# Normalisation moved from VectorE to ScalarE, low parts moved within a unit, and a bias folded into the products of a graph pass

## The chip, the cores and the metric

The kernel runs on one core of a Trainium2 chip. The metric is the device time of one execution in microseconds (us); lower is better. Three executions of the kernel before were timed, and one more was taken with the hardware profiler.

## The reference

`x` is 128 graphs of 64 nodes with 384 features, `adj` is 128 matrices of 64x64. Four layers follow each other, each as `x = layernorm(x + layer(x, adj))`:

- Layers 0 and 3: attention with 12 heads over the 64 nodes of a graph; the adjacency (twice it in layer 0) is added to the scaled scores; then an output projection with its bias.
- Layer 1: attention with 12 heads, `beta * adj` added, scores where `adj` is not over 0 masked; no output projection.
- Layer 2: two inner layers of a graph network. Each takes `softmax(h h^T / sqrt(384)) * adj`, normalised by its row sums, as `attn`, and

```
ctx = (attn * upper) @ (h Wl^T + bl) + diag(attn) * (h Ws^T + bs) + (attn * lower) @ (h Wr^T + br)
h = relu(layernorm(ctx) * g + beta)
```

All is float32.

## The kernel before

The 8192 rows are cut into 16 groups of 512 rows, and a group into 4 units of 128 rows (two graphs). There are five passes over all rows, one after the other, with a barrier of all engines between them: `attention_pass` for layer 0 (first pass), for layer 1 (second pass), `digcn_pass` for the two inner layers (first and last graph pass), and `attention_pass` for layer 3 (last pass). Rows go to memory between passes. Each pass writes its own queue for every engine by hand: a function `group(i, pair, par)` per engine lists, unit by unit (`s` = 0 to 3, `n` the unit's number), what the engine does, and the engines meet at semaphores. Within an engine's queue everything is done in the order written. Most operands have two buffers, `b` = 0 and 1.

Products are made of a high and a low part: every matrix and every row block is rounded to the format of the fast matmul (the high part, an operation of ScalarE) and what the rounding loses is kept as a second matrix (the low part, a subtraction). A product is then nine matmuls, three over the depth for each of high-high, low-high and high-low (`SPLIT`).

In an attention pass a unit `n` goes this way:

- PE: `scores(n)` (L471), `values(n-2)` (L505 or L509), the transposes of the probabilities `probs_T(n-1)` (L484), the output projection `output(n-2)` (L524, where `wo` is set: first and last pass), and between them the ten projections of the next group (`ahead`, L444 and L450), spread over the four units by `BETWEEN`. They wait for the next group's high and low parts.
- DVE (VectorE): `residual(n-3)` (L807 adds the rows, L811 and L814 take mean and variance), `softmax_max(n)` (L751, L758, in first and last pass L760), `low_part(n-2)` (L794 or L798), `normed(n-3)` (L823: subtract the mean, multiply by the inverse deviation), in unit 2 `edges` (L738, L740 or L743), `softmax_sum(n)` (L765 to L780), then transposes of later rows (L717) and, in first and last pass, their low parts (L723).
- POOL (GpSimd): `rstd(n-3)` (L339, L341: the inverse deviation), the subtraction of the maximum (L387), `value_bias(n)` (L347); in the second pass then `add_rows(n-2)` (L366) and `rows_low` (L372: in unit 2 two low parts, in unit 3 one); in first and last pass `output_bias` (L355) and the multiplication L398, which waits for L776.
- ACT (ScalarE): evacuates the projections from PSUM, `exp(n)` (L656), `probs_T` (L651), `values` (L666), high parts (L584).
- The SP queue loads rows and stores `yo`; a store waits for the normalisation of its unit.

In a graph pass (`digcn_pass`; `ends` is true in the last one alone) a unit `n` goes this way:

- PE: projections LEFT and RIGHT (L1165), `context(n-1)` (L1179), in unit 1 `products` of the next group (L1138, they wait for the transposes L1332), the projection SELF (L1165), in unit 3 `attention_T` of the next group (L1149, it waits for L1372).
- DVE: `itself(n-1)` (L1386: SELF plus its bias row into `hs`), transposes (L1332: unit 0 one, units 2 and 3 one each), in unit 3 attention steps 3 and 4 (L1366, L1372, L1377, L1379: the last makes `diag`), `inner_norm` (L1412 to L1425 if `ends`, else L1428 and L1434), `context(n-1)` (L1398: `hs * diag + ps_c`, then L1401 and L1404), in unit 1 step 0, in unit 2 steps 1 and 2 (L1352, L1355, L1358, L1361).
- ACT: `left_right` (L1242), high parts, exp, `standardise(n-2)` (L1259) and `normed(n-4)` (L1267) if `ends`, else `relu`.
- POOL: inverse deviations (L1070 to L1076), low parts (L1085), `side_biases` (L1092), attention steps (L1052, L1058).

## Time and profile before

| | |
|---|---|
| median of 3 runs | 2729.84 us (2726.38 to 2730.54) |
| profiled execution | 2732.55 us |
| its span, first to last instruction | 2730.8 us |
| mean granted clock of TensorE | 0.966 |
| PE busy | 2468.6 us (90%) |
| DVE busy | 2263.7 us (83%) |
| POOL busy | 1895.4 us (69%) |
| ACT busy | 1456.9 us (53%) |
| DMA, mean | 74 GB/s |

Busy time is given per engine over the whole span; the passes have different limits, so the shares are averages over five unlike stages. The view of windows gives the same for a stretch, the view of the timeline gives single instructions with their start and duration in us and, in square brackets, the idle time of their engine just before them and what ended it. An arrow `out<-in` names the operands; `l_` stands for the pass.

### The profile page before, as it was taken

The page shows a single profiled execution, that of the slowest core. Times are in us where ns is not written, and L with a number is a line of the kernel's source. Part 1 is how long each engine was busy: PE and PEld are TensorE (multiplying, and loading weights), DVE is VectorE, ACT ScalarE, POOL GpSimd, SP SyncE. Part 2 cuts the span into 40 slices and gives each one's busy share as a digit, 9 for nine tenths or more (in the row PEclk, how much of TensorE's full clock was granted, in tenths as well). Part 3 has the DMA queues.
Part 4 walks back from the last instruction along what each step waited for, and adds up shares of the span by engine and source line. Part 5 has one row for each costly group of instructions (what it writes and reads, how often), then busy time and mean ns, then how long its engine had stood idle before and what let it go on. Part 6 is the DMA issues. An engine that isn't in the chain of part 4 may idle for free. (4 is left out here: it accounts for less than half of the span.)

```text
span 2730.8 us, 64297 instructions
## 1 busy us (share of the span) xinstructions
PE 2468.6 (90%) x21490; PEld 2094.7 (77%) x21490; DVE 2263.7 (83%) x3822; ACT 1456.9 (53%) x2964; POOL 1895.4 (69%) x2093
## 2 busy tenths in 40 slices
PE   6999999995999999959999978998895999999997
PEld 5888888874877777748888867777774788888886
DVE  5999999984788888867777769889897699999997
ACT  4555555552666666535544545555554555555553
POOL 2777777773677777756666647788784577777776
PEclk9999999997999999979999989999997999999999
DMA  7222222115233332163332163333324222222211
GB/s 133 62 66 70 70 66 70 47 46 104 63 80 76 90 76 66 54 125 72 73 67 64 50 114 83 89 91 76 92 65 95 49 66 70 67 68 70 58 45 51
DMA packets 320740, 200.89 MB, mean 74 GB/s; under 512 B 243440, under 2 KB 320624, under 8 KB 320624
## 3 DMA queue, kind: packets, MB, share of 16 engines
q1 hardware_dynamic: 320624, 199.40, 31.6%
q8 instruction: 66, 1.08, 0.2%
q14 instruction: 50, 0.41, 0.0%
HBM read 136.42 MB, written 62.91 MB: 73 GB/s over the span
## 5 line engine op out<-in xcount | busy, mean ns | idle before, releaser
L450 PE MATMUL l_ps_p<-l_xT,l_w 128*128 128x512 f32 x2304 | 602.7, 409 | 99.6 <-POOL l_xT L372 50.4
L1165 PE MATMUL l_ps_h<-l_w,l_hT 128*128 128x384 f32 x3456 | 658.1, 345 | 10.1 <-DVE l_hs L1386 7.3
L1165 PEld LDWEIGHTS l_ps_h<-l_w,l_hT 128*128 128x128 f32 x3456 | 607.1, 191 | 74.0 <-issue 42.4
L450 PEld LDWEIGHTS l_ps_p<-l_xT,l_w 128*128 128x128 f32 x2304 | 430.9, 193 | 197.1 <-issue 102.2
L387 POOL TENSOR_TENSOR l_pr<-l_sc,l_st 128x768 f32<-128x768 f32 x192 | 283.1, 1475 | 328.8 <-DVE l_st L758 327.6
L347 POOL TENSOR_TENSOR v<-v,l_bvs 128x768 f32<-128x768 f32 x192 | 375.6, 1956 | 0.0
L1242 ACT ACTIVATE l_hlr<-l_ps_h 64x384 f32<-64x384 f32 x512 | 248.8, 486 | 228.3 <-PE l_ps_h L1165 219.1
L1092 POOL TENSOR_TENSOR l_hlr<-l_hlr,l_sides 128x768 f32<-128x768 f32 x128 | 240.1, 1876 | 119.9 <-ACT l_hlr L1242 119.9
L444 PE MATMUL l_ps_p<-l_w,l_xT 128*128 128x384 f32 x1584 | 311.2, 342 | 0.0
L615 ACT ACTIVATE v<-l_ps_p 64x192 f32<-64x192 f32 x704 | 228.6, 325 | 142.0 <-PE l_ps_p L444 135.3
L765 DVE TENSOR_REDUCE l_st<-l_pr 128x12 f32<-128x768 f32 x192 | 182.7, 952 | 126.9 <-ACT l_pr L656 125.7
L524 PE MATMUL l_ps_y<-l_w,l_oT 128*128 128x384 f32 x1152 | 237.6, 352 | 47.2 <-DVE l_oT L798 43.5
L444 PEld LDWEIGHTS l_ps_p<-l_w,l_xT 128*128 128x128 f32 x1584 | 273.1, 188 | 5.8 <-issue 0.2
L524 PEld LDWEIGHTS l_ps_y<-l_w,l_oT 128*128 128x128 f32 x1152 | 204.6, 193 | 80.9 <-issue 77.3
L398 POOL TENSOR_TENSOR l_pr<-l_pr,l_st 128x768 f32<-128x768 f32 x128 | 211.1, 1649 | 38.0 <-DVE l_st L776 28.6
L656 ACT ACTIVATE l_pr<-l_pr 128x768 f32<-128x768 f32 x192 | 163.1, 850 | 85.4 <-POOL l_pr L387 81.4
L751 DVE SCALAR_TENSOR_TENSOR l_sc<-l_ps_s,l_sbias 128x768 f32<-128x768 f32 x192 | 183.6, 956 | 30.1 <-PE l_ps_s L471 22.3
L651 ACT ACTIVATE l_pT<-l_ps_t 128x512 f32<-128x512 f32 (+1 forms) x384 | 167.5, 490 | 50.0 <-PE l_ps_t L484 44.4
L758 DVE TENSOR_REDUCE l_st<-l_sc 128x12 f32<-128x768 f32 x192 | 183.0, 953 | 6.7
L605 ACT ACTIVATE l_k<-l_ps_p,even_odd 128x512 f32<-128x512 f32 x192 | 121.7, 685 | 110.9 <-PE l_ps_p L450 110.9
L471 PE MATMUL l_ps_s<-l_k,l_qT 64*64 64x128 f32 x4608 | 172.1, 280 | 5.3 <-DVE l_sc L751 5.3
L484 PE MATMUL l_ps_t<-ident,l_pr 128*128 128x128 f32 x1152 | 165.5, 281 | 12.6 <-POOL l_pr L398 9.5
(127 smaller groups left out, 4297.9 us busy)
## 6 DMA issues: line engine op xcount, KB each, us to landing
rows<-l_yo SPq DMA_DIRECT2D x256, 192.0 KB, 1.9
l_xa<-rows SPq DMA_DIRECT2D x256, 192.0 KB, 4.3
l_xr<-rows SPq DMA_DIRECT2D x192, 192.0 KB, 2.4
l_xa<-in_x SPq DMA_DIRECT2D x64, 192.0 KB, 4.2
l_xr<-in_x SPq DMA_DIRECT2D x64, 192.0 KB, 2.4
out<-l_yo SPq DMA_DIRECT2D x64, 192.0 KB, 1.9
l_edge<-in_adj SPq DMA_DIRECT2D x80, 128.0 KB, 2.4
raw<-in_L_gnn_Wq SPq DMA_DIRECT2D x12, 144.0 KB, 4.8
```

Source lines behind the costliest of these rows:

```text
L347: nc.gpsimd.tensor_tensor(got, got, bvs[:, :, :].unsqueeze(1).to_broadcast([P, GPU, PAIRS, 64]), ALU.add).then_inc(pool_v, 1)
L387: nc.gpsimd.tensor_tensor(pr[b][:, :, :], sc[b][:, :, :], st[b][:, 0, :].unsqueeze(2).to_broadcast([P, HEADS, NODES]), ALU.subtract).then_ ...
L398: nc.gpsimd.tensor_tensor(pr[b][:, :, :], pr[b][:, :, :], st[b][:, 5, :].unsqueeze(2).to_broadcast([P, HEADS, NODES]), ALU.mult).then_inc( ...
L444: last = nc.tensor.matmul(bank[:, :D], rows[:, l, t, o * P:(o + 1) * P], W[2][:, r, t, :], start=c + t == 0, stop=c == 2 and t == KT - 1)
L450: last = nc.tensor.matmul(bank[:, :], W[m][:, l, t, o * P:(o + 1) * P], rows[:, r, t, :], start=c + t == 0, stop=c == 2 and t == KT - 1)
L524: last = nc.tensor.matmul(ps_y[:, :D], oT[b][:, l, t, :], W[3][:, r, t, :], start=c + t == 0, stop=c == 2 and t == KT - 1)
L615: i = nc.scalar.activation(v2[gpar][64 * odd:64 * odd + 64, GPU * u + g2, :, 32 * odd:32 * odd + 32], got[:, :, odd, :], ACT.Copy)
L751: nc.vector.scalar_tensor_tensor(out=sc[b][:, :, :], in0=logits[:, :, :NODES], scalar=scale, in1=sbias[par][:, s, :].unsqueeze(1).to_broad ...
L758: nc.vector.tensor_reduce(st[b][:, 0, :], sc[b][:, :, :], AX.X, ALU.max).then_inc(dve_mx, 1)
L1092: nc.gpsimd.tensor_tensor(hlr[b][:, :, :], hlr[b][:, :, :], sides[:, :, :], ALU.add).then_inc(pool_h, 1)
L1165: last = nc.tensor.matmul(ps_h[m][:, :D], hT[gpar][:, l, t, s * P:(s + 1) * P], W[m][:, r, t, :], start=c + t == 0, stop=c == 2 and t == K ...
L1242: i = nc.scalar.activation(hlr[b][half * NODES:(half + 1) * NODES, g, :], ps_h[m][g * NODES:(g + 1) * NODES, :D], ACT.Copy)
```

## The change

- All three attention passes: `normed` leaves DVE's queue and becomes three operations on ACT, which stand behind `exp(n)` and the evacuations next to it, and ahead of `rows_high`. The store and the reuse of `res` wait for ACT instead of DVE.
- Second pass: `rows_low` on POOL stands behind `rstd(n-3)` at the head of units 2 and 3, ahead of the subtraction of the maximum. In first and last pass low parts stay on DVE as they were.
- Last graph pass: the bias row of SELF is added by a tenth matmul (a matrix `pick` with rows 0 and 32 set to one, times a matrix `bias` whose rows 0 and 32 hold the high and the low part of the bias); ACT multiplies the result by `diag` while it reads it from PSUM into `hs`; DVE's `itself` is gone and its context sum is a plain addition.
- Both graph passes: DVE's order within a unit. In the last one it is context, attention steps 3 and 4, inner norm, transpose, steps 0 to 2; in the first one `itself`, steps 3 and 4, inner norm, context, transpose, steps 0 to 2.
- At the start of the kernel DVE fills `pick`.

The diff, cut to its core:

```diff
@@ constants, DVE
+                nc.vector.memset(self.pick[:, :].bitcast(F32), 0.0).then_inc(c_pick, 1)
+                dve.wait_ge(c_pick, 1)
+                dve.wait_ge(c_const, 5)
+                for row in (0, 32):
+                    nc.vector.tensor_copy(self.pick[row:row + 1, :], self.ones[row:row + 1, :]).then_inc(c_const, 1)
@@ attention_pass, POOL
                     rstd(n - 3, 1 - b)
+                    for t in ((), (), (0, 1), (2,))[s]:
+                        rows_low(i + 2, par, t)
                     pool.wait_ge(dve_mx, n + 1)
...
                         add_rows(n - 2, pair * 4 + 2 * par + s // 2 - 1, b)
-                        for t in ((), (), (0, 1), (2,))[s]:
-                            rows_low(i + 2, par, t)
@@ attention_pass, ACT
+            def normed(n, count, b):
+
+                if not inside(n, units):
+                    return
+                act.wait_ge(dve_mv, n + 1)
+                nc.scalar.activation(ln[b][:, 10:11], ln[b][:, 6:7], ACT.Copy, scale=-1.0).then_inc(act_nm, 1)
+                act.wait_ge(pool_rs, n + 1)
+                act.wait_ge(act_nm, 2 * n + 1)
+                nc.scalar.activation(ln[b][:, 11:12], ln[b][:, 10:11], ACT.Copy, scale=ln[b][:, 9:10]).then_inc(act_nm, 1)
+                act.wait_ge(act_nm, 2 * n + 2)
+                if counted(16 * count):
+                    act.wait_ge(s_out[b], 16 * count)
+                nc.scalar.activation(yo[b][:, :], res[b][:, :], ACT.Identity, bias=ln[b][:, 11:12],
+                                     scale=ln[b][:, 9:10]).then_inc(act_y, 1)
...
                         exp(n, s % 2)
                         fill(i, par, s, 1)
+                    normed(n - 3, pair * 4 + 2 * par + (s - 3) // 2, 1 - s % 2)
                     for t in ((), (0, 1), (2,), ())[s]:
                         rows_high(i + 2, par, t)
@@ attention_pass, DVE
                     low_part(n - 2, s % 2)
-                    normed(n - 3, count, 1 - s % 2)
@@ digcn_pass, PE
+                if ends and m == SELF:
+                    if isinstance(n, int) and n == 0:
+                        pe.wait_ge(c_row, 2)
+                    last = nc.tensor.matmul(ps_h[m][:, :D], pick[:, :], bias[:, :], start=False, stop=True)
@@ digcn_pass, ACT
                     normed(n - 4, pair * 4 + 2 * par + s // 2 - 2, b)
+                    if ends:
+                        act.wait_ge(pe_h, 3 * n + 3)
+                        act.wait_ge(dve_dg, i + 1)
+                        if counted(n - 1):
+                            act.wait_ge(dve_c, n - 1)
+                        nc.scalar.activation(hs[b][:, :], ps_h[SELF][:, :D], ACT.Copy,
+                                             scale=diag[par][:, s:s + 1]).then_inc(act_h, 1)
@@ digcn_pass, DVE
+                if ends:
+                    dve.wait_ge(act_h, 3 * (n + 1))
+                    nc.vector.tensor_tensor(c0[b][:, :], ps_c[:, :D], hs[b][:, :], ALU.add).then_inc(dve_c, 1)
...
+            if ends:
+                dve.wait_ge(act_w, steps + 1)
+                nc.vector.tensor_tensor(bias[32:33, :], brow[32:33, :], bround[32:33, :].bitcast(F32),
+                                        ALU.subtract).then_inc(c_row, 1)
...
+                    before = (i, par, s - 1) if s else (i - 1, 1 - par, UNITS - 1)
+                    if ends:
+                        context(n - 1, *before)
                     itself(n - 1, 1 - b)
+                    if s == 3:
+                        attention(i + 1, 1 - par, 3)
+                        attention(i + 1, 1 - par, 4)
+                    if ends:
+                        inner_norm(n - 3, pair * 4 + 2 * par + (s - 3) // 2, 1 - b)
+                    else:
+                        inner_norm(n - 2, pair * 4 + 2 * par + s // 2 - 1, b)
+                        context(n - 1, *before)
```

## Rows read from the trace of the kernel before

**Rows 1.** Windows, busy us of PE, PEld, DVE, ACT, POOL; passes one to four.
```profile
200.00:571.20 371.20, 361.37 (x3427) 306.29 (x3425) 339.46 (x551) 208.49 (x440) 272.36 (x241) 1.00 0.25 63
...
800.00:1049.00 249.00, 233.89 (x2422) 194.81 (x2422) 216.92 (x295) 153.84 (x317) 192.19 (x183) 0.99 0.33 80
...
1300.00:1497.00 197.00, 197.00 (x1408) 170.97 (x1407) 149.52 (x297) 98.68 (x200) 129.41 (x137) 1.00 0.31 69
...
1750.00:1981.00 231.00, 206.35 (x1404) 175.09 (x1403) 207.73 (x387) 128.21 (x231) 187.39 (x326) 0.97 0.35 84
```

**Rows 2.** Timeline (start us, duration us) of the first pass, one unit, DVE and POOL.
```profile
352.69 0.61 DVE L823 TENSOR_SCALAR l_yo<-l_res,l_ln 128x384 f32<-128x384 f32 x1
353.99 0.95 DVE L765 TENSOR_REDUCE l_st<-l_pr 128x12 f32<-128x768 f32 x1 [0.70 <-ACT l_pr L656]
...
355.24 0.76 DVE L776 SCALAR_TENSOR_TENSOR l_st<-l_st 128x12 f32<-128x12 f32 x1
...
353.04 1.97 POOL L347 TENSOR_TENSOR v<-v,l_bvs 128x768 f32<-128x768 f32 x1
354.97 1.02 POOL L355 TENSOR_TENSOR l_xr<-l_xr,l_bos 128x384 f32<-128x384 f32 x1
```

**Rows 3.** Timeline of POOL in the first unit of the first pass.
```profile
51.30 1.85 POOL L347 TENSOR_TENSOR v<-v,l_bvs 128x768 f32<-128x768 f32 x1
```

**Rows 4.** Groups of ACT by line (count, busy us, mean ns), the two graph passes.
```profile
L1259 ACT ACTIVATE l_c<-l_c,l_ln 128x384 f32<-128x384 f32 x64 | 45.1, 704 | 48.9 <-POOL l_ln L1076 48.7
...
L1251 ACT ACTIVATE l_yo<-l_c 128x384 f32<-128x384 f32 x64 | 33.0, 515 | 13.6 <-DVE l_c L1434 13.6
```

**Rows 5.** Timeline of the second pass, end of a group, POOL, DVE and PE.
```profile
920.43 1.48 POOL L387 TENSOR_TENSOR l_pr<-l_sc,l_st 128x768 f32<-128x768 f32 x1 [1.24 <-DVE l_st L758]
...
923.76 1.06 POOL L366 TENSOR_TENSOR l_res<-l_scaled,l_xr 128x384 f32<-128x384 f32 x1
...
926.14 0.50 DVE L811 BATCH_NORM_STATS2 l_ln<-l_res 128x6 f32<-128x384 f32 x1
...
933.36 1.25 POOL L372 TENSOR_TENSOR l_xT<-l_xF,l_xT 128x512 fp32r<-128x512 f32 x1
...
934.75 4.44 PE L450 MATMUL l_ps_p<-l_xT,l_w 128*128 128x512 f32 x18 [2.13 <-POOL l_xT L372]
```

**Rows 6.** Timeline of DVE in the last graph pass, units 0, 2 and 3.
```profile
1856.15 0.52 DVE L1412 TENSOR_TENSOR l_c<-l_c,l_gain 128x384 f32<-128x384 f32 x1
...
1858.97 0.62 DVE L1398 SCALAR_TENSOR_TENSOR l_c<-l_hs,l_diag,l_ps_c 128x384 f32<-128x384 f32 x1
...
1860.41 0.56 DVE L1386 TENSOR_TENSOR l_hs<-l_ps_h,l_own 128x384 f32<-128x384 f32 x1
...
1872.31 0.39 DVE L1352 TENSOR_REDUCE l_st<-l_u 128x4 f32<-128x256 f32 x1
...
1873.53 1.34 DVE L1358 SCALAR_TENSOR_TENSOR l_st<-l_st 128x4 f32<-128x4 f32 x1
...
1875.01 0.56 DVE L1386 TENSOR_TENSOR l_hs<-l_ps_h,l_own 128x384 f32<-128x384 f32 x1
...
1876.11 0.90 DVE L1366 TENSOR_TENSOR l_attn<-l_u,l_st 128x256 f32<-128x256 f32 x1
1877.04 0.70 DVE L1372 TENSOR_TENSOR l_wide<-l_attn,l_halves 128x512 f32<-128x512 f32 x1
```

**Rows 7.** Timeline of PE in the last graph pass, the context products of three units.
```profile
1862.01 0.87 PE L1179 MATMUL l_ps_c<-l_hlr,l_aT 128*64 128x384 f32 x4
...
1869.09 0.87 PE L1179 MATMUL l_ps_c<-l_hlr,l_aT 128*64 128x384 f32 x4
...
1874.90 0.54 PE L1179 MATMUL l_ps_c<-l_hlr,l_aT 128*64 128x384 f32 x2
```

**Rows 8.** Timeline of PE and DVE at the start of the last graph pass.
```profile
1625.81 0.60 PE L1149 MATMUL l_ps_a<-ident,l_wide 128*128 128x128 f32 x4
...
1626.68 0.52 DVE L1386 TENSOR_TENSOR l_hs<-l_ps_h,l_own 128x384 f32<-128x384 f32 x1
```

More of the change, by code:

```diff
@@ L904, in digcn_pass @@
         loaded = list(shared.loads)
-        own = a.sb("own", [P, D])
+        own = None if ends else a.sb("own", [P, D])
+        if ends:
+            pick = shared.pick
+            brow = a.sb("brow", [P, D])
+            bround = a.sb("bround", [P, D], F32R)
+            bias = a.sb("bias", [P, D], F32R)
+            c_zero, c_row = a.sem("c_zero"), a.sem("c_row")
         sides = a.sb("sides", [P, GPU, D])
@@ L982, in _ @@
             sp.dma_start(edge[0][:, :, :], adj_g[0]).then_inc(s_edge[0], 16)
-            sp.dma_start(own[:, :], row_biases[SELF].to_broadcast([P, D])).then_inc(s_small, 16)
+            if ends:
+                for row in (0, 32):
+                    sp.dma_start(brow[row:row + 1, :], row_biases[SELF]).then_inc(s_small, 16)
+            else:
+                sp.dma_start(own[:, :], row_biases[SELF].to_broadcast([P, D])).then_inc(s_small, 16)
             for g in range(GPU):
@@ L1157, in project @@
                     pe.wait_ge(dve_w, KT * (m + 1))
-                if m == SELF:
+                if m == SELF and not ends:
                     if counted(n):
                         pe.wait_ge(dve_s, n)
-                elif counted(2 * (n - 1) + m + 1):
-                    pe.wait_ge(act_h, 2 * (n - 1) + m + 1)
+                elif counted(taken * (n - 1) + m + 1):
+                    pe.wait_ge(act_h, taken * (n - 1) + m + 1)
                 for c, (l, r) in enumerate(SPLIT):
@@ L1381, in itself @@
             def itself(n, b):
-                if not inside(n, units):
+                if ends or not inside(n, units):
                     return
@@ L1435, in inner_norm @@
                                                op0=ALU.mult, op1=ALU.add).then_inc(dve_o, 1)
+            if ends:
+                nc.vector.memset(bias[:, :].bitcast(F32), 0.0).then_inc(c_zero, 1)
             weights(LEFT)
@@ L1479, in _ @@
             itself(units - 1, 1)
+            context(units - 1, groups - 1, 1, UNITS - 1)
             if ends:
                 inner_norm(units - 3, units // 2 - 2, 1)
-            context(units - 1, groups - 1, 1, UNITS - 1)
             inner_norm(units - 2, units // 2 - 1, 0)
```

64 lines of the change are left out of this document (31 added, 33 removed).

## The prediction, made before the changed kernel was run

> **What bounds the kernel now.** I first read busy time in one steady stretch of each pass [rows 1], each of whole groups (a group is four 128-row units): 371.2/10 = 37.1 us a group in the first pass, 249/8 = 31.1 in the second, 197/8 = 24.6 in the first graph pass, 231/8 = 28.9 in the last. The last pass repeats the first (37.1). TensorE is busy 361.37 of 371.2, all of 197, but only 206.35 of 231. So the first graph pass is bound by TensorE, and a faster VectorE gives nothing there; the last graph pass does the same products with 4.3 us a group more, and VectorE is busy 207.73 of 231.
>
> Then the order in time of one unit of the first pass [rows 2]. VectorE never waits for TensorE in it; it waits 0.70 us for ScalarE's exp (L765). That wait closes a chain: maximum on VectorE, subtraction on GpSimd, exp on ScalarE, sum on VectorE. The normalisation (L823) stands inside that wait. The second thing to see is L776: a 128x12 operation that takes 0.76 us and ends at 356.00, when GpSimd's L355 (354.97 + 1.02) ends at 355.99. GpSimd's sequence after the maximum sets VectorE's next step, so VectorE's busy share hides two waits, not one.
>
> In the second pass TensorE waits 2.13 us once a group for the low part L372, which ends at 934.61 [rows 5]. It looks like the prize, but no wait of VectorE for TensorE stands in the steady stretch: TensorE idles because VectorE's and GpSimd's chain paces it.
>
> **Part 1: normalisation to ScalarE (three passes, 192 units).** Off VectorE goes L823. In units 0, 1, 3 of a group the exp wait grows by what is removed: 0.70 becomes about 1.3, gain 0. What does transfer is small: GpSimd's L347 takes 1.97 behind L823 [rows 2] and 1.85 in the first unit, where there is no L823 yet [rows 3]. L355 and L776 come 0.12 earlier. In unit 1 that is lost, as TensorE's and ScalarE's evacuations lead into unit 2's exp; units 0 and 3 keep it: 2 x 0.12 x 32 groups of the first and last pass = -7.7. Bounds: 0 and 3 x 0.12 x 32 = -11.5.
>
> On ScalarE come three operations: a 128x384 one with scale and bias columns, 0.704, of which the same size without them is 0.515 [rows 4]; and two of one element per partition, priced between 0 and 0.515 each, and taken as 0.2, as most of the 384 elements are gone. With two waits on its own results, some 0.15 together, about 1.25 us a unit, 240 us in all. In the first pass ScalarE is busy 208.49 of 371.2 [rows 1]; with 40 x 1.25 = 50 more it is idle less and is not full. The normalisation stands behind exp, so it can't delay it; behind it are queued the high parts and the last evacuation of the unit. I take nothing for it; if the cover is gone, the excess is paid twice a group. Against it speaks the Trainium skill, "ScalarE: Activation LUTs", section "Rules for kernel authors", which puts adds and multiplies on VectorE, not ScalarE. By its rule the exchange is a loss in busy time (the trace agrees: 0.704 against 0.61); what decides is the wait that covers it.
>
> Ends: at the end of each attention pass the last store waits for 0.2 + 0.704 instead of 0.61 on the path: 3 x 0.3 = +0.9.
>
> **Part 2: low parts at a unit's head in the second pass.** The two or one L372 (1.25 each, [rows 5]) move ahead of GpSimd's subtraction L387 in units 2 and 3. In unit 2 that one waits 1.24 us for the maximum, 2.5 us of low parts go in, so the subtraction is 1.3 us late, and with it exp, value bias and L366. L366 now ends at 924.82, its reader L811 starts at 926.14: the slack of 1.3 us is used up exactly. VectorE's own way to L811 leads through the edge operations, whose two also wait for GpSimd; with L823 gone they start 1.5 earlier. In unit 3 1.25 us meet a similar wait. Unit 2: +0.2, unit 3: 0, less 0.1 for the faster L347. Sum 0. TensorE's 2.13 us wait goes, and comes back elsewhere as it waits for exp. Bounds: -0.5 and +2.0 us a group (no slack used at all), -8 to +32.
>
> **Part 3: last graph pass.** VectorE loses the bias addition L1386 (0.56) four times a group, 2.2 us, and the context sum becomes a plain addition, 0.05 cheaper: 2.4 a group. ScalarE gains one scaled read of PSUM, 4 x 0.6, onto 128.21/8 = 16.0; TensorE one more matmul a unit, which at 5.81 for a unit's 31 [rows 7] is 0.19, 0.8 a group. If VectorE's sum were all, the group would be 26.5. But the order changes too: context first, then attention steps 3 and 4, inner norm, and the transpose last. Where a product starts the next context, waits close a loop across engines. I add it up from TensorE's context of unit 2:
> - context to VectorE's start 0.9;
> - context 1.45 (1858.97 to 1860.41), inner norm 2.82 (1856.15 to 1858.97), its wait for GpSimd's side biases 0.7, transpose 0.63, attention 1 and 2 at 1.5: L1352 starts at 1872.31 and L1386 at 1875.01, 2.70, of which L1358 holds 1.34 where it needs about 0.16 [rows 6]; together 7.1;
> - in unit 3 context 1.45 and L1366, L1372 at 1.15 (1876.11 to 1877.74 is 1.63 with a stall): 2.6;
> - TensorE's attention transpose and two projections: 4.0;
> - unit 0 to 1: 5.81 (1869.09 to 1874.90) + 0.19; unit 1 to 2: 7.08 (1862.01 to 1869.09) + 0.19 [rows 7]; 13.3.
>
> Sum 27.9, against 28.9: -1.0 x 16 = -16. TensorE then waits for `wide` instead of for the context. Bounds: 26.5 (-38) and, with L1358 stalled as in [rows 6] and more, 29.6 (+11). I take 27.9 as it has every stall but the one that hangs on a few hundredths.
> At its start VectorE subtracts the bias row behind its transposes, at about 1626.7, and TensorE's attention transpose, which stood at 1625.81 [rows 8], follows unit 0's SELF product: +1.3 with the waits.
>
> **Part 4: nothing.** In the first graph pass the transpose moves behind the context; TensorE is full there [rows 1] and needs it a unit later. The constants at the start of the kernel: +0.5 (0 to 1).
>
> **Sum:** -7.7 - 16 + 0.9 + 1.3 + 0.5 = -21. Profiled execution 2732.55 (span 2730.8 and 1.75 around it), so 2711.5; it stood 2.7 above the median 2729.84, so 2709. 0.2% is 5.5 us, about what a measurement can tell here.
>
> **Rivals.**
> A, forecast, 54%.
> B, the stall in the last graph pass. L1358, 1.34 us in [rows 6], is issued in my schedule within 0.1 us of GpSimd's side biases. If it comes second, the group is 29.6 and `wide` later: -21 + 27 = +6, 2736. For it: L776 in [rows 2] shows the same waiting to the end of another engine's operation. The Trainium skill, "SBUF — State Buffer", section "Who interferes with whom", says the same: an operation of VectorE with two SBUF inputs and one of GpSimd exclude each other, and issue order decides. 14%.
> C, the loop isn't closed and VectorE's sum counts: 26.5 a group, -38 in place of -16, 2687. For it: in the old order VectorE hardly waits for TensorE there. Against it: the new order ties `wide` to the context. 17%.
> D, slower: in the second pass the late subtraction isn't hidden. It decides where L366 ends later than L780, from 1.3 us a group on, which eats the 21; at 2.0 us a group +32, so +11, 2741. Against it the slack counted above. 10%.
> E, slower too: ScalarE is late. At the upper bounds the three operations take 0.704 + 2 x 0.515 and some 0.3 of waits, 2.0 us rather than 1.25, and the evacuations queued behind them come late; 0.75 x 2 x 48 groups = +72, less 21, 2781. Against it: ScalarE is idle 44% of the first pass. 5%. The page on ScalarE named in part 1 has the rule that leads here.
> That the diff doesn't do what its title says I see no room for, beside that "stay" means no edit.
>
> **Numbers.** Faster: C and nearly all of A, 70%. Same: half of B, the edge of A and D, 13%. Slower: 17%. The range 2683 to 2737 takes in A, B and C and leaves D and E out.
>
> **What would show it.** First pass: L765's wait near 1.3 where it was 0.70, L347 at 1.85, group 36.9. Second: group 31.1 still, no wait for L372, L811 waiting for L366. Last graph pass: group 27.9, TensorE waiting for L1372's successor, no wait for the context sum. Wrong: the second pass shorter by over 0.5 us a group (then TensorE did pace it), or the graph pass near 26.5 or 29.6.

## The result, and the profile after

The changed kernel is slower: 2750.48 us (2749.3 to 2753.89, four runs) against 2728.54 us (2726.38 to 2730.54, four runs) of the kernel before on the same chip, a ratio of 1.0081, 95% interval 1.0069 to 1.0093. The forecast was 2709, range 2683 to 2737. Of the two profiled executions the spans differ by 18.1 us (2730.8 and 2748.9), as the one before stood some 4 us above its median.

The page of the kernel after: span, and busy time of each engine.
```profile
span 2748.9 us, 65175 instructions
...
PE 2478.1 (90%) x21554; PEld 2101.8 (76%) x21554; DVE 2095.0 (76%) x3571; ACT 1698.2 (62%) x3606; POOL 1878.9 (68%) x2093
```
VectorE was given less to do, and nothing gained by it. To see where the time went I cut the span at ScalarE's exp instructions, 64 in each attention pass (their starts in the timeline):

| stretch, us | before | after |
|---|---|---|
| start to first exp | 51.5 | 50.8 |
| first pass, exp 1 to 64 | 574.1 | 582.4 |
| to the second pass | 65.9 | 64.7 |
| second pass, exp 1 to 64 | 487.1 | 481.4 |
| both graph passes | 956.7 | 965.9 |
| last pass, exp 1 to 64 | 577.4 | 584.1 |
| to the end | 18.1 | 19.6 |

So three stretches lost (8.3, 9.2 and 6.7 us), one gained (5.7). How much such a stretch varies by itself is read from the kernels below in which its pass is as before: 573.8 to 574.1 us for the first pass, 487.1 to 488.4 for the second, 956.4 to 958.1 for the graph passes, 574.3 to 577.4 for the last. Windows of the kernel after that answer to the first, second and last of [rows 1] (PE, PEld, DVE, ACT, POOL, granted clock):
```profile
200.00:571.20 371.20, 355.52 (x3396) 301.54 (x3395) 308.54 (x503) 250.07 (x553) 263.32 (x237) 1.00 0.25 62
...
800.00:1049.00 249.00, 234.81 (x2451) 193.40 (x2450) 173.89 (x265) 188.82 (x417) 191.11 (x185) 1.00 0.34 80
...
1750.00:1981.00 231.00, 209.22 (x1363) 178.89 (x1362) 187.03 (x350) 137.60 (x257) 184.79 (x317) 0.96 0.35 83
```
In the first and last of these TensorE got through fewer matmuls than in [rows 1], 3396 against 3427 and 1363 against 1404; in the second through more, 2451 against 2422.

**First pass.** Timeline of VectorE and GpSimd in one unit after, the counterpart of [rows 2]. L791 was L765, L796, L799 and L802 were L770, L773 and L776, L354 and L362 were L347 and L355.
```profile
358.21 0.95 DVE L791 TENSOR_REDUCE l_st<-l_pr 128x12 f32<-128x768 f32 x1 [1.23 <-ACT l_pr L663]
359.08 1.02 DVE L796 SCALAR_TENSOR_TENSOR l_st<-l_st 128x12 f32<-128x12 f32 x1
360.02 0.21 DVE L799 RECIPROCAL l_st<-l_st 128x12 f32<-128x12 f32 x1
360.27 0.17 DVE L802 SCALAR_TENSOR_TENSOR l_st<-l_st 128x12 f32<-128x12 f32 x1
...
357.25 1.84 POOL L354 TENSOR_TENSOR v<-v,l_bvs 128x768 f32<-128x768 f32 x1
359.04 1.04 POOL L362 TENSOR_TENSOR l_xr<-l_xr,l_bos 128x384 f32<-128x384 f32 x1
```
The value bias L354 takes 1.84 us and not 1.97, as forecast. So the output bias L362 begins at 359.04, and VectorE's 128x12 operation L796, issued at 359.08, lasts until that one ends: 1.02 us. The row of the same operation in the kernel before stands between those of [rows 2]:
```profile
354.86 0.17 DVE L770 SCALAR_TENSOR_TENSOR l_st<-l_st 128x12 f32<-128x12 f32 x1
```
In both kernels the sum begins 0.95 us behind the value bias (0.96 after) and the small operation 1.82 us behind it (1.83 after). But the output bias began 1.93 us behind it before and begins 1.79 us behind it now. Before, the first two of the three got through and only the last was caught (0.76 us, of which 0.6 waiting); now the first is caught and the other two follow it, and the last of them ends 3.19 us behind the start of the value bias instead of 2.96.

This is not one unit's accident. In each of the two passes 45 of the 64 units have the output bias beside that small operation (units 0, 1 and 3 of a group). Before, VectorE's was issued first in all 90, by 0.12 us at most (mostly 0.10), and took 0.16 to 0.18 us. After, it was issued second in all 90, by 0.01 to 0.09 us, and took 0.96 to 1.04.

**Second pass.** Unit 2 of a group after: GpSimd's low parts L379 (L372) and subtraction of the maximum L396 (L387), VectorE's maximum L784, sum L791 and the first operation of the variance, L839 (L811).
```profile
924.15 2.55 POOL L379 TENSOR_TENSOR l_xT<-l_xF,l_xT 128x512 fp32r<-128x512 f32 x2
926.65 1.53 POOL L396 TENSOR_TENSOR l_pr<-l_sc,l_st 128x768 f32<-128x768 f32 x1
...
924.31 0.95 DVE L784 TENSOR_REDUCE l_st<-l_sc 128x12 f32<-128x768 f32 x1
...
929.10 0.95 DVE L791 TENSOR_REDUCE l_st<-l_pr 128x12 f32<-128x768 f32 x1 [0.63 <-ACT l_pr L663]
...
931.19 0.56 DVE L839 BATCH_NORM_STATS2 l_ln<-l_res 128x6 f32<-128x384 f32 x1 [0.88 <-POOL l_res L373]
```
The maximum is there at 925.26; the subtraction starts 1.39 us later, behind the low parts, and VectorE waits for exp even in the unit of the edge operations. Then it waits 0.88 us more for GpSimd's addition of the rows (L373, before L366): what rival D of the prediction described.

**Last graph pass.** Timeline of VectorE and TensorE at a group's turn after (L1445 was the context sum L1398, L1410 and L1416 the attention steps L1366 and L1372, L1176 the attention transpose L1149), three windows over it, and from the views of TensorE's and of VectorE's waits between 1800 and 1980 us the largest of each.
```profile
1912.21 0.56 DVE L1445 TENSOR_TENSOR l_c<-l_ps_c,l_hs 128x384 f32<-128x384 f32 x1
...
1913.57 0.54 DVE L1410 TENSOR_TENSOR l_attn<-l_u,l_st 128x256 f32<-128x256 f32 x1
1914.14 0.70 DVE L1416 TENSOR_TENSOR l_wide<-l_attn,l_halves 128x512 f32<-128x512 f32 x1
...
1914.89 0.66 PE L1176 MATMUL l_ps_a<-ident,l_wide 128*128 128x128 f32 x4 [2.48 <-DVE l_wide L1416]
1915.75 4.96 PE L1192 MATMUL l_ps_h<-l_w,l_hT 128*128 128x384 f32 x18 [0.20 <-issue]
```
```profile
1913.00:1916.00 3.00, 0.90 (x5) 0.67 (x6) 2.79 (x8) 0.73 (x2) 2.73 (x5) 0.97 0.00 0
1916.00:1919.00 3.00, 3.00 (x10) 3.00 (x10) 2.43 (x5) 0.18 (x1) 0.78 (x3) 0.50 0.19 49
1919.00:1922.00 3.00, 3.00 (x16) 2.15 (x16) 0.27 (x1) 2.87 (x6) 0.30 (x2) 0.96 0.22 82
```
```profile
PE l_ps_a L1176 <- DVE l_wide L1416: 14.4, 6, 2.5
...
DVE l_c L1445 <- PE l_ps_c L1211: 14.2, 13, 2.9
```
The same view of TensorE's waits in the kernel before:
```profile
PE l_ps_c L1179 <- DVE l_c L1398: 10.5, 6, 1.9
...
PE l_ps_a L1149 <- DVE l_wide L1372: 1.5, 6, 0.3
```
The wait of 0.25 us for `wide` has become one of 2.48, since the context sum now stands in front; the wait for the context sum is gone. Behind this wait the granted clock is 0.50, the lower of its two levels (1.2 GHz), and 18 matmuls take 4.96 us; such a row of 18 takes 3.29 at a clock of 1.00. And VectorE, which takes the context sum first, now stands waiting for TensorE's context (14.2 us). A group, from one attention transpose to the next, takes 29.8 us on average; by the same reading it was 29.2 before, not the 28.9 that the prediction took from a window. The clock doesn't fall in each group: of ten between 1720 and 2020 us it does in seven. These seven take 30.1 us on average, the three at a clock of 1.00 take 29.1 (the one from 1886.09 to 1914.89 takes 28.8, the next one, with this fall, 30.6). The kernel before has such falls too, in six of ten groups, behind its waits of 1.6 to 1.9 us for the context sum; I had not looked. But they cost nothing there: its groups take 28.9 and 29.5 us in turn, whether the clock falls in them (28.91 from 1760.98, 29.52 from 1848.27) or not (28.89 from 1877.79, 29.50 from 1965.08).

### The profile page after: what moved, and what is told of

It is laid out like the page before. It is cut to its first block and busy times, and to the rows that moved or that the text cites. A ratio compares the mean times of both kernels' runs of the same rounds, so it can differ in the third digit from the quotient of the medians.

```text
span 2748.9 us, 65175 instructions
## 1 busy us (share of the span) xinstructions
PE 2478.1 (90%) x21554; PEld 2101.8 (76%) x21554; DVE 2095.0 (76%) x3571; ACT 1698.2 (62%) x3606; POOL 1878.9 (68%) x2093
## 5 line engine op out<-in xcount | busy, mean ns | idle before, releaser
L1192 PE MATMUL l_ps_h<-l_w,l_hT 128*128 128x384 f32 x3456 | 671.5, 347 | 2.2 <-issue 2.0
L1192 PEld LDWEIGHTS l_ps_h<-l_w,l_hT 128*128 128x128 f32 x3456 | 614.0, 193 | 63.3 <-issue 53.9
L457 PEld LDWEIGHTS l_ps_p<-l_xT,l_w 128*128 128x128 f32 x2304 | 425.2, 191 | 175.9 <-issue 86.0
L396 POOL TENSOR_TENSOR l_pr<-l_sc,l_st 128x768 f32<-128x768 f32 x192 | 284.0, 1479 | 298.9 <-DVE l_st L784 298.9
L791 DVE TENSOR_REDUCE l_st<-l_pr 128x12 f32<-128x768 f32 x192 | 182.9, 953 | 289.5 <-ACT l_pr L663 289.5
L354 POOL TENSOR_TENSOR v<-v,l_bvs 128x768 f32<-128x768 f32 x192 | 358.0, 1865 | 0.0
L1119 POOL TENSOR_TENSOR l_hlr<-l_hlr,l_sides 128x768 f32<-128x768 f32 x128 | 249.1, 1946 | 123.3 <-ACT l_hlr L1274 122.8
L784 DVE TENSOR_REDUCE l_st<-l_sc 128x12 f32<-128x768 f32 x192 | 183.0, 953 | 6.6
L478 PEld LDWEIGHTS l_ps_s<-l_k,l_qT 64*64 64x64 f32 x4608 | 125.9, 134 | 64.7 <-issue 58.0
```

The source lines that it names most:

```text
L354: nc.gpsimd.tensor_tensor(got, got, bvs[:, :, :].unsqueeze(1).to_broadcast([P, GPU, PAIRS, 64]), ALU.add).then_inc(pool_v, 1)
L396: nc.gpsimd.tensor_tensor(pr[b][:, :, :], sc[b][:, :, :], st[b][:, 0, :].unsqueeze(2).to_broadcast([P, HEADS, NODES]), ALU.subtract).then_ ...
L457: last = nc.tensor.matmul(bank[:, :], W[m][:, l, t, o * P:(o + 1) * P], rows[:, r, t, :], start=c + t == 0, stop=c == 2 and t == KT - 1)
L478: last = nc.tensor.matmul(logits[g * NODES:(g + 1) * NODES, h:h + 2, :NODES], qT[par][q, t, c:c + NODES], k2[par][q, t, :, c:c + NODES], s ...
L1119: nc.gpsimd.tensor_tensor(hlr[b][:, :, :], hlr[b][:, :, :], sides[:, :, :], ALU.add).then_inc(pool_h, 1)
L1192: last = nc.tensor.matmul(ps_h[m][:, :D], hT[gpar][:, l, t, s * P:(s + 1) * P], W[m][:, r, t, :], start=c + t == 0, stop=not (ends and m = ...
```

## The experiments

Each was timed in five rounds beside the kernel before, which took 2730.8 us beside e1 to e4, 2729.4 beside e5, e7, e8 and e9, and 2730.3 beside the rest. The ratio is to these. The columns of the table are the stretches of the one above: first pass, second pass, both graph passes, last pass.

| kernel | us | ratio (95% interval) | first | second | graph | last |
|---|---|---|---|---|---|---|
| e1_norm | 2725.77 | 0.9982 (0.9973 to 0.9991) | 582.0 | 468.6 | 956.6 | 583.7 |
| e2_low | 2731.57 | 1.0000 (0.9991 to 1.0009) | 574.0 | 488.6 | 956.9 | 575.8 |
| e3_graph | 2741.64 | 1.0034 (1.0021 to 1.0048) | 573.8 | 488.1 | 968.5 | 575.8 |
| e4_wide_first | 2743.89 | 1.0043 (1.0030 to 1.0057) | 574.0 | 488.2 | 970.4 | 574.4 |
| e5_old_order | 2713.97 | 0.9938 (0.9925 to 0.9952) | 573.9 | 487.2 | 939.6 | 575.3 |
| e6_bias_ahead | 2703.77 | 0.9903 (0.9887 to 0.9918) | 562.6 | 488.4 | 958.1 | 564.7 |
| e7_norm_bias_ahead | 2685.95 | 0.9837 (0.9823 to 0.9850) | 563.8 | 468.7 | 956.4 | 562.9 |
| e8_later_T | 2729.30 | 0.9997 (0.9988 to 1.0006) | 573.8 | 487.6 | 954.7 | 575.7 |
| e9_norm_mid | 2710.48 | 0.9928 (0.9915 to 0.9942) | 573.8 | 469.2 | 957.5 | 574.3 |
| e10_best | 2670.06 | 0.9782 (0.9769 to 0.9796) | 562.7 | 468.2 | 940.9 | 563.8 |
| e11_low_back | 2739.38 | 1.0031 (1.0018 to 1.0043) | 582.3 | 468.1 | 971.2 | 584.1 |
| e12_spare | 2711.38 | 0.9928 (0.9915 to 0.9942) | 573.9 | 468.3 | 956.5 | 574.3 |

### Single parts of the change: e1_norm, e2_low, e3_graph

**e1_norm**
```diff
 # before, attention_pass, DVE
-                    normed(n - 3, count, 1 - s % 2)
 # ACT, behind exp
+                    normed(n - 3, pair * 4 + 2 * par + (s - 3) // 2, 1 - s % 2)
```


> Of the change only the normalisation on ScalarE in the three attention passes; low parts and graph passes as before. Theory T1 (the whole of the loss in the first and last pass is this part: GpSimd's value bias runs in 1.85 us instead of 1.97, its output bias then starts just ahead of VectorE's subtraction m0, which waits it out at about 1.02 us instead of 0.17, and the sum over heads and the residual follow later): first and last pass +7 to +9 us each (a group 37.1 to about 37.6), second pass between -3 and 0, both graph passes unchanged; whole kernel +9 to +17 us, 2738 to 2746. Rival (the loss in these passes is something else, and the part gives what was forecast): -8 us, 2721. Rival (ScalarE is late with the evacuations behind its three new instructions): also slower, but then PE waits for ScalarE's evacuations grow and m0 stays at 0.17.

Measured 2725.77: 5 us faster, so T1's time for the whole kernel (9 to 17 us slower) was missed, and the rival's gain of 8 us was not reached. The first and last pass lost 7.9 and 6.3 us, about as T1 had it. The second pass gained 18.5, which neither theory had. Its cause stands in unit 2 of a group. First the kernel before, VectorE's timeline, then ScalarE's exp:
```profile
920.64 1.47 DVE L823 TENSOR_SCALAR l_yo<-l_res,l_ln 128x384 f32<-128x384 f32 x1
922.04 1.92 DVE L738 TENSOR_SCALAR l_off<-l_edge 128x256 f32<-128x256 f32 x1
923.99 1.11 DVE L740 SCALAR_TENSOR_TENSOR l_sbias<-l_edge,l_betas,l_off 128x256 f32<-128x256 f32 x1
925.02 0.94 DVE L765 TENSOR_REDUCE l_st<-l_pr 128x12 f32<-128x768 f32 x1
...
921.93 0.85 ACT L656 ACTIVATE l_pr<-l_pr 128x768 f32<-128x768 f32 x1 [1.05 <-POOL l_pr L387]
```
The same of e1_norm, where the edge operations are L757 and L759, the sum L784:
```profile
948.28 1.40 DVE L757 TENSOR_SCALAR l_off<-l_edge 128x256 f32<-128x256 f32 x1
949.72 1.95 DVE L759 SCALAR_TENSOR_TENSOR l_sbias<-l_edge,l_betas,l_off 128x256 f32<-128x256 f32 x1
951.59 0.94 DVE L784 TENSOR_REDUCE l_st<-l_pr 128x12 f32<-128x768 f32 x1
...
949.57 0.85 ACT L656 ACTIVATE l_pr<-l_pr 128x768 f32<-128x768 f32 x1 [0.70 <-POOL l_pr L387]
```
In this unit VectorE doesn't wait for exp: its own work holds the sum up, until 2.24 us after exp's end before (922.78 to 925.02) and 1.17 after it now (950.42 to 951.59). 1.07 us a group times 16 is 17 of the 18.5. And L823 took 1.47 us there, until 0.2 us behind the end of GpSimd's L387 (921.91, [rows 5]). So it was a wait too. The 0.61 of [rows 2] holds a shorter one: there also L823 ends 0.21 us behind the end of L387 (353.09), and in the last three units of each attention pass, where no operation of GpSimd overlaps it, it takes 0.48. The Trainium skill, "SBUF — State Buffer", section "Who interferes with whom", says that an operation of this kind, one tensor with scalars, can take the pair of ports that VectorE shares with GpSimd; the rows agree (1.47 us beside L387, 0.48 with nothing beside it).

**e2_low**
```diff
 # before, attention_pass, POOL
                     rstd(n - 3, 1 - b)
+                    for t in ((), (), (0, 1), (2,))[s]:
+                        rows_low(i + 2, par, t)
                     pool.wait_ge(dve_mx, n + 1)
...
                         add_rows(n - 2, pair * 4 + 2 * par + s // 2 - 1, b)
-                        for t in ((), (), (0, 1), (2,))[s]:
-                            rows_low(i + 2, par, t)
```


> Of the change only the subtraction of the low parts at the head of a unit in the second pass; everything else as before. Theory: TensorE's wait of 2.13 us for the last low part goes, the group stays within 0.3 us of 31.1; the second pass between -6 and +1 us, the other stages unchanged, whole kernel 2722 to 2730. Rival D of the prediction (the add of the rows comes late behind the subtractions): second pass +8 or more, 2737 or more.

Measured 2731.57, within a microsecond of before; the second pass took 488.6 us, 0.5 more than in e3_graph and e4_wide_first, where it is untouched. The wait for the low part went (15.1 us in eight waits between 800 and 1049 us before), waits for ScalarE and VectorE came in its place (7.1 and 6.6 us), and nothing was gained, as forecast. The range stated was missed by 1.6 us, the mechanism held.

**e3_graph**
```diff
 # attention passes as before; Shared and digcn_pass as after
+                    if ends:
+                        context(n - 1, *before)
```


> Attention passes as before; the last graph pass (and what it shares) as in the changed kernel: the bias as a matmul, the scaling on ScalarE, the new order on VectorE. Theory T2: TensorE waits 2.2 to 2.6 us a group for the transpose wide, which now stands behind the context sum on VectorE, and after that wait its granted clock falls to between 0.6 and 0.8; a group 30.1 instead of 28.9, whole kernel +8 to +11 us, 2737 to 2740. Rival (the last graph pass only suffers from the state in which the attention pass leaves the cores): the pass is faster than before here, 2712 to 2725.

Measured 2741.64, 11 us more and 1.6 above the range of T2, all in the graph stretch (968.5 against 956.7). A group takes 29.9 us, TensorE waits 2.3 to 2.7 for `wide`, and the clock falls in eight of ten groups. The rival, that the pass suffers from something before it, falls. The three parts alone come to -5, +1 and +11 us, +7 in all; the change cost 22. So two of them don't add up.

### Why the first and last pass lost: e12_spare, e7_norm_bias_ahead, e6_bias_ahead

**e12_spare**
```diff
 # e1_norm, first and last pass, DVE, at the old place
+                nc.vector.tensor_scalar(spare[b][:, :], res[b][:, :], ln[b][:, 6:7], ln[b][:, 9:10], ALU.subtract,
+                                        ALU.mult).then_inc(dve_spare, 1)
```


> As e1_norm, and in the first and last pass VectorE also computes the normalisation at its old place, into a spare tile that nobody reads: 61 instructions of 0.61 us more in each of these passes, while ScalarE keeps its three new ones. Theory T1 (the passes are longer because without that instruction GpSimd's value bias ends 0.12 us earlier and the output bias is under way before m0 is issued): value bias 1.97 us again, m0 at 0.17, the first and last pass back at 574 and 575 us though VectorE does more; whole kernel 2709 to 2716. Rival (ScalarE's three instructions are what is late): the passes stay at 582 and 584 us or grow by VectorE's 0.6 us a unit, 2724 or more.

Measured 2711.38, 14 us faster than e1_norm with 122 instructions more. Timeline of VectorE (L845 writes the spare tile, L790 is the small operation) and GpSimd (L348 value bias, L356 output bias):
```profile
352.34 0.61 DVE L845 TENSOR_SCALAR l_spare<-l_res,l_ln 128x384 f32<-128x384 f32 x1
...
354.52 0.17 DVE L790 SCALAR_TENSOR_TENSOR l_st<-l_st 128x12 f32<-128x12 f32 x1
...
352.69 1.96 POOL L348 TENSOR_TENSOR v<-v,l_bvs 128x768 f32<-128x768 f32 x1
354.62 1.01 POOL L356 TENSOR_TENSOR l_xr<-l_xr,l_bos 128x384 f32<-128x384 f32 x1
```
The small operation is again 0.10 us ahead of the output bias instead of 0.04 behind it, and the passes are back at 573.9 and 574.3. ScalarE has its three new instructions here too; so it isn't ScalarE. A useless instruction, worth 0.61 us of VectorE's time a unit, pays for itself by making GpSimd's value bias 0.12 us longer.

**e7_norm_bias_ahead**
```diff
 # e1_norm, attention_pass, POOL
                     rstd(n - 3, 1 - b)
+                    output_bias(n - 2, pair * 4 + 2 * par + s // 2 - 1, b)
                     pool.wait_ge(dve_mx, n + 1)
...
-                    output_bias(n - 2, pair * 4 + 2 * par + s // 2 - 1, b)
                     pool.wait_ge(dve_rinv, n + 1)
```


> As e1_norm, and in the first and last pass GpSimd's output bias stands ahead of its wait for the maximum instead of behind the value bias. Theory T1: the subtraction m0 that e1_norm holds up for about 1.0 us and the two instructions behind it are free (m0 at 0.17 us), the first and the last pass lose the 6 to 8 us that e1_norm added and up to 12 us more each; whole kernel 2686 to 2714. Rival (the passes are late for ScalarE's three new instructions and not for the collision): the passes stay at e1_norm's 582 and 584 us, 2722 or more. Rival (the bias ahead of the wait delays GpSimd's subtraction of the maximum by its 1.0 us): slower than e1_norm, 2735 or more.

Measured 2685.95, at the lower edge of T1's range (2686). The output bias (L355) now runs in GpSimd's idle time, and nothing meets the small operations (L789 is the first of them). Timeline of POOL and DVE, and the only line that the view of TensorE's waits has between 210 and 560 us:
```profile
352.67 1.01 POOL L355 TENSOR_TENSOR l_xr<-l_xr,l_bos 128x384 f32<-128x384 f32 x1
...
358.90 0.16 DVE L789 SCALAR_TENSOR_TENSOR l_st<-l_st 128x12 f32<-128x12 f32 x1
```
```profile
PE l_ps_y L524 <- DVE l_oT L817: 3.2, 9, 0.4
```

**e6_bias_ahead**: the same move in the kernel before, the normalisation still on VectorE.


> The kernel before with one change: in the first and last pass GpSimd's output bias stands ahead of its wait for the maximum. Theory T1 (the gain of e7 is the collision of the output bias with the three small VectorE instructions, of which before only the last, 0.6 us over its own length, was caught): units 0, 1 and 3 of a group 0.4 to 0.7 us shorter, the two passes 8 to 20 us less each, whole kernel 2692 to 2714. Rival (the order gains only with the normalisation off VectorE): within 4 us of before, 2725 to 2733.

Measured 2703.77, in the range of T1, and the rival falls: the passes take 562.6 and 564.7 us. Against e7 (563.8, 562.9) the normalisation's place makes no difference to them once the collision is gone; TensorE bounds them then: it is busy 346.6 of the 350 us between 210 and 560 in both. The whole of what the change cost in these passes, and 12 us a pass beyond it, lay in where GpSimd adds 128x384 numbers.

### The second pass: e9_norm_mid, e11_low_back

**e9_norm_mid**: `normed` on ScalarE where `wo` is not set, on VectorE where it is.


> Of the change only the normalisation on ScalarE, and that in the second attention pass alone; all else as before. Since e1_norm lost 8 and 6 us in the first and last pass and gained 18.5 us in the second: second pass 467 to 471 us between its first and last unit (487.1 before), first and last pass as before (574, 577), whole kernel 2708 to 2716. Rival (the second pass gains because the first leaves it another state): second pass over 480, 2724 or more.

Measured 2710.48; the second pass took 469.2. The gain is the pass's own.

**e11_low_back**
```diff
 # after, attention_pass, POOL
                     rstd(n - 3, 1 - b)
-                    for t in ((), (), (0, 1), (2,))[s]:
-                        rows_low(i + 2, par, t)
                     pool.wait_ge(dve_mx, n + 1)
...
                         add_rows(n - 2, pair * 4 + 2 * par + s // 2 - 1, b)
+                        for t in ((), (), (0, 1), (2,))[s]:
+                            rows_low(i + 2, par, t)
```


> The changed kernel with one part undone: in the second pass the low parts are subtracted at a unit's end again. Theory (with the normalisation off VectorE, the two low parts at the head of unit 2, which wait for the variance and hold up the subtraction of the maximum by 1.4 us, are what eats the second pass's gain): second pass 468 to 470 us instead of 481, whole kernel 2735 to 2741. Rival (the parts add up, as alone the low parts at the head were worth nothing): second pass stays at 480 or more, 2747 or more.

Measured 2739.38, and 468.1 in place of 481.4 in the second pass: 13.3 us, 0.83 a group. The kernel gained 11.1 only. Its graph stretch, whose code is that of the changed kernel, came out at 971.2 instead of 965.9, and e3_graph has 968.5: with the new order this stretch varies by some 5 us. The same edit is worth nothing in e2_low and 13 us here. With L823 on VectorE the sum of unit 2 was late by VectorE's own work, and the late subtraction was hidden by it; without L823 the subtraction ends the wait: in e2_low the sum of unit 2 still begins 1.2 us behind exp's end on average, in the changed kernel it follows exp at once. This is the interaction that the single parts didn't show: of the 15 us that they leave open it is 13 in the pass's own time and 11 in the kernel's. The rest is open.

### The last graph pass: e4_wide_first, e5_old_order, e8_later_T

**e4_wide_first**
```diff
 # e3_graph, digcn_pass, DVE
-                    if ends:
-                        context(n - 1, *before)
                     if s == 3:
                         attention(i + 1, 1 - par, 3)
                         attention(i + 1, 1 - par, 4)
+                    if ends:
+                        context(n - 1, *before)
```


> As e3_graph, but in VectorE's last unit of a group the two attention steps that end in wide stand ahead of the context sum. Theory T2 (the late wide and the clock after it are the whole cost): the wait for wide falls under 0.6 us, the granted clock stays near 1.00 over the group's turn, a group 27.0 to 28.2, 14 to 38 us less than e3_graph less what the context sum now brings; whole kernel 2700 to 2722. Rival (the bias matmul and ScalarE's scaling are the cost): a group stays at 29.5 or more, 2733 or more. Rival (the context sum becomes the wait, of 1.6 us or more, in wide's place): 28.5 to 29.5 a group, 2725 to 2733.

Measured 2743.89, a group 30.3 us: my T2 missed. The number fits the rival that the bias matmul and the scaling cost by themselves, but the trace shows another cause. GpSimd (L1110, the side biases), VectorE and TensorE at a group's turn:
```profile
1882.56 1.81 POOL L1110 TENSOR_TENSOR l_hlr<-l_hlr,l_sides 128x768 f32<-128x768 f32 x1
...
1882.86 1.79 DVE L1401 TENSOR_TENSOR l_attn<-l_u,l_st 128x256 f32<-128x256 f32 x1
1884.69 0.69 DVE L1407 TENSOR_TENSOR l_wide<-l_attn,l_halves 128x512 f32<-128x512 f32 x1
...
1885.44 1.11 PE L1167 MATMUL l_ps_a<-ident,l_wide 128*128 128x128 f32 x4 [2.29 <-DVE l_wide L1407]
```
The attention step, issued 0.30 us behind the side biases, takes 1.79 us instead of the 0.54 that it took at 1913.57 after. What the move wins, it loses to the collision; TensorE's wait is again 2.29. Over ten groups, the time that VectorE's operations take beyond the shortest of their kind is 6.6 us a group, in e3_graph 4.3; its idle time is 3.9 and was 5.7. The clock is not the cost here: it falls in seven of these groups, and the other three take 30.1 to 30.4 us all the same.

**e5_old_order**: e3_graph, with VectorE's order of the kernel before (transposes, attention steps 3 and 4, inner normalisation, context sum last).


> As e3_graph (bias as a matmul, scaling on ScalarE in the last graph pass, attention passes as before), but VectorE takes its work in the order of the kernel before: transposes, the attention steps that end in wide, the inner normalisation, and the context sum last. Theory T3 (from e4: it is not the order of wide and context sum, but VectorE as a whole that reaches wide late, because its products with two SBUF inputs, gain, shift, attention weights and wide, run into GpSimd's adding of the side biases, 1.8 us, in every unit): with the old order the collisions fall elsewhere; the wait for wide is under 0.6 us, TensorE waits for the context sum 1.5 to 2 us as before, a group 28.0 to 29.0, whole kernel 2715 to 2732. Rival (the bias matmul and the scaling on ScalarE cost by themselves, whatever the order): a group 29.5 or more, 2738 or more.

Measured 2713.97, 27.7 us less than e3_graph and 1 below the range of T3, a group 28.1. Timeline of VectorE (L1436 is the context sum) and TensorE, a window over a group, TensorE's waits from 1800 to 1980:
```profile
1915.23 0.56 DVE L1436 TENSOR_TENSOR l_c<-l_ps_c,l_hs 128x384 f32<-128x384 f32 x1
...
1920.70 1.26 DVE L1407 TENSOR_TENSOR l_wide<-l_attn,l_halves 128x512 f32<-128x512 f32 x1
...
1922.07 0.60 PE L1167 MATMUL l_ps_a<-ident,l_wide 128*128 128x128 f32 x4
```
```profile
1895.00:1923.00 28.00, 25.62 (x182) 22.11 (x181) 24.14 (x46) 17.70 (x33) 22.88 (x41) 1.00 0.38 89
```
```profile
PE l_ps_c L1202 <- DVE l_c L1436: 7.9, 6, 1.5
PE l_ps_c L1202 <- POOL l_hlr L1110: 7.4, 11, 0.8
```
The context sum of unit 2 is out of the way before unit 3 begins; `wide` is ready at 1921.96, when TensorE comes for it. TensorE's waits are several small ones (1.55 us at most), and the granted clock falls in none of the ten groups. The bias matmul and the scaling, kept here, are the gain of the part; the new order was its loss. T3's reason doesn't hold, though: VectorE's operations take 4.7 us a group beyond the shortest of their kind, not less than in e3_graph (4.3). What fell is VectorE's idle time, from 5.7 to 3.5 us a group.

**e8_later_T**
```diff
 # e3_graph, digcn_pass, PE
                     project(n, i, par, s, LEFT)
+                    if ends and s == 0 and counted(i):
+                        attention_T(i)
                     project(n, i, par, s, RIGHT)
...
-                    if s == 3:
+                    if s == 3 and not ends:
```


> As e3_graph, but TensorE takes the transposes of wide nine matmuls (1.7 us) later, behind the left projection of the next group. Theory T2/T3 (what costs is TensorE standing idle 2.2 to 2.6 us a group for wide, and the lower clock that follows): the wait falls to 0.4 to 1.0 us, the clock stays near 1.00, a group 27.8 to 28.8; whole kernel 2705 to 2725. Rival (VectorE is the engine that bounds the pass now, so the wait comes back at another place): a group stays at 29.5 or more, 2735 or more.

Measured 2729.30, a group 29.0: between both expectations, so T2 holds for a part only. The granted clock falls in no group, as there, but the wait for `wide` is still 1.3 to 1.9 us, and a second one of 1.3 to 2.0 stands at the products of the rows (L1156, for VectorE's transpose). Without the falls the pass is 0.9 us a group faster than e3_graph (29.9), where e5_old_order is 1.8 faster; the other half I put down to VectorE's order. There VectorE waits for TensorE's context at a unit's head, with everything else behind it. How the two share it more exactly stays open, since the later transpose shifts VectorE's inputs too.

### The parts that gain, together: e10_best

Normalisation on ScalarE, output bias ahead of the maximum, low parts at the unit's end, graph part as e5.


> The parts that gained, together: normalisation on ScalarE in all three attention passes with the output bias ahead of the maximum (e7), low parts at a unit's end, and the last graph pass with the bias matmul and ScalarE's scaling in VectorE's old order (e5). If the parts are independent, as stages that follow each other should be: 2685.95 less 15.4 us, 2666 to 2675. Rival (the passes disturb each other): over 2678.

Measured 2670.06, ratio 0.9782 (0.9769 to 0.9796), where the sum of the parts gave 2670.5. It beats both kernels: 60 us below the one before, 80 below the changed one.

## Why the prediction was wrong

- **Part 1, first and last pass.** The exp wait (1.23, forecast "about 1.3") and the value bias (1.84, forecast 1.85) came as written. The step that failed is "L355 and L776 come 0.12 earlier". L355 did; but I moved L776 with it and didn't ask what stood between them. L770, at 354.86 in the trace, was 0.11 us ahead of L355, and 0.12 us is more than that. Forecast -7.7 for the two passes, measured +7.9 and +6.3 (e1_norm). The rest of the step held: from exp to exp, units 0 and 3 pass the shift on (9.07 to 9.40 us, 8.55 to 8.84, averages of ten groups of the first pass), unit 1 and unit 2 don't (9.67 and 9.83 in both). The row needed stood between two that I quoted. I had named this very mechanism for L1358 in the graph pass (rival B) and not for the operation that it hit.
- **Part 1, second pass.** I took nothing. The step that failed is the general one, that what leaves VectorE only lengthens the wait for exp: in unit 2 there is no such wait, and L823 cost 1.47 us there, not 0.61. Part 2 of the prediction has the clue, that with L823 gone the edge operations start 1.5 us earlier; part 1 didn't price it. Measured -18.5.
- **Part 1, ScalarE.** The groups of ScalarE after, first pass, mean ns:
```profile
L688 ACT ACTIVATE l_yo<-l_res,l_ln 128x384 f32<-128x384 f32 x39 | 27.6, 709 | 3.3
L684 ACT ACTIVATE l_ln<-l_ln 128x1 f32<-128x1 f32 x39 | 11.5, 295 | 2.5
L681 ACT ACTIVATE l_ln<-l_ln 128x1 f32<-128x1 f32 x39 | 7.6, 194 | 0.2
```
  1.20 us a unit, forecast 1.1 and 0.15 of waits. Rival E fell: e12_spare and e7_norm_bias_ahead carry the same three and lose nothing by them.
- **Part 2.** Forecast 0, bounds -8 to +32: alone 0 (e2_low), with part 1 +13.3. Rival D was the right mechanism: the subtraction is 1.39 us late where 1.3 was forecast, and VectorE waits 0.88 us for L373, which was L366. My slack for it was a slack of the kernel before; part 1 used it up. (The group of this pass took 31.45 us before, as an average of ten, and not the 31.1 of the window.) D was priced without part 1's gain in the same pass, so the pass as a whole came out 5.7 us faster and not slower.
- **Part 3.** Forecast 27.9 a group, measured 29.8; the graph stretch +9.2 where -16 + 1.3 was forecast. The forecast that TensorE would wait for `wide` instead of the context was right. The schedule missed 1.9 us a group. The step that failed is the sum of the loop, which left two things out.

  One is the clock behind that wait: 18 matmuls in 4.96 us and not 3.29, in seven groups of ten. As these groups are 1.0 longer than the others (30.1 against 29.1), it comes to 0.7 a group.

  The other is 1.2 that are missing even at full clock (29.1 against 27.9). In the group of 28.8, TensorE goes from its attention transpose to the next context product in 3.7 us (4.0 in the sum), on to the one in unit 1 in 5.9 (6.0), to the one in unit 2 in 8.0 (7.3), and from there to the next attention transpose in 11.2 (10.6). In the last of these VectorE's wait at the unit's head was 1.0, and 0.9 was priced; but its inner normalisation took 4.2, where I had 2.82 and a stall of 0.7. Its shift addition (L1463) ran into GpSimd's side biases (L1119), as their timeline shows:
```profile
1906.71 2.09 DVE L1463 TENSOR_TENSOR l_c<-l_c,l_shift 128x384 f32<-128x384 f32 x1
...
1906.22 2.17 POOL L1119 TENSOR_TENSOR l_hlr<-l_hlr,l_sides 128x768 f32<-128x768 f32 x1
```
  On the way to unit 2 TensorE's products waited 0.50 us for VectorE's transpose, which stood behind a wait of 0.87 for the context and a gain multiplication that took 1.79 instead of 0.55; the sum had no such wait. No run tells the waits at a unit's head and the collisions wholly apart, but e3_graph against e5_old_order speaks for the waits: VectorE's idle time is 5.7 us a group against 3.5, the time lost in collisions and like delays 4.3 against 4.7.

  With the old order the bias matmul and ScalarE's scaling give 28.1 a group and -17 us in the stretch (e5_old_order): what I had forecast for the new order. Rival B's price, 29.6, was near by chance: its L1358 ran undisturbed (0.16 us at 1911.74), and other operations were caught. The bias matmul was priced rightly: two context products stand 5.89 us apart where they stood 5.71 (0.19 forecast). Rival C's 26.5 a group was not reached by any order tried; 28.1 was the best.
- **Part 4.** Nothing was forecast for the first graph pass, and nothing came: 384.5 us from its first to its last context product in both kernels.
- **Ends and constants.** +0.9 forecast for the ends, the last stretch grew by 1.5; +0.5 for the constants, -0.7 measured. From the last context product of the first graph pass to the first of the last one it is 1.3 more, as forecast.

Of the 39 us between the forecast's -21 and the spans' +18, 23 are the first and last pass and 24 the graph passes; the second pass gave 6 back, and the ends and gaps 2.

## What to carry to other kernels

Where VectorE and GpSimd hand over to each other within a few tenths of a microsecond, list every VectorE operation with two SBUF inputs (and every scaling of one tensor) on either side of the hand-over and its distance to GpSimd's next start; an edit that shifts one side by more than the smallest distance can change who waits, and the sign of the edit with it. The cure here was not a faster operation but a place: the movable GpSimd operation belongs where VectorE is in single-input or PSUM work. Price an edit in every unit of the period, not in the typical one, and try parts together as well as alone, since a slack can be used only once.

## What the runs showed of the hardware

- A 128x12 operation of 0.17 us took 1.02 when GpSimd's 128x384 addition had been started 0.04 us before it, and 0.17 when it came 0.10 us ahead. Nothing lies between: in the 90 units where the two meet it was first 90 times in the kernel before, once by as little as 0.001 us, and took 0.18 at most; in the changed kernel it was second 90 times, and took 0.96 at least. The same page and section of the Trainium skill as above has it that the issue order decides and the later one waits for the whole operation; these rows agree.
- It holds for VectorE's scaling of one tensor by two columns as well: 1.47 us in the second pass, 0.61 in the first, each time until 0.2 us behind the end of GpSimd's subtraction, and 0.48 with nothing beside it.
- TensorE's granted clock fell to 0.50 (1.2 GHz) for some 3 us behind waits of 1.6 to 2.9 us, but not behind each: the same 2.34 us were followed by 0.50 at 1765 us and by 1.00 at 1886 in the kernel after. In the last graph pass it fell in six groups of ten before, seven after, and in none of e5_old_order (longest wait 1.55 us) and e8_later_T (2.03). What decides besides the last wait's length these runs don't show. In the kernel after, the groups with a fall are 1.0 us longer than those without; in the kernel before they are not longer at all.
